# W_k's loads on another queue, W_o's low parts on another engine, projections one step earlier, the last tile in halves

## What is computed

```
x = x + o_mod(attention(k_mod(x)))     # q = k = v = x * style_k @ W_k.T * demod + b, 16 heads of 32
                                       # scores between the heads of one token, not between tokens
x = x + x @ (U V)[:-1] + (U V)[-1]     # weight of rank 30, made from cond by W_dec
x = x + clip(mod(x, W_2), -256, 256)   # a third modulated product
x = x + LN(silu(cat @ W1 + b1) @ W2 + b2) * g + be
#   cat = [h, t, m, n, r, s], each weighted: two chained LNs with gathered rows (h), two LNs with
#   gathered rows (t, s), x plus the output of a small MLP (m, n, r)
```

## Time and profile before

| what | value |
|---|---|
| three runs | 1007.46, 1013.16, 1014.13 us; median 1013.16 |
| the profiled execution | 1011.57 us, its span 1009.8 us |
| PE, DVE, ACT, POOL busy | 979.1, 662.7, 489.9, 693.9 us |
| DMA engines in 0 to 33 us | busy 0.97, 304 GB/s |
| PE busy in 61 to 70 us | 9.00 of 9 us |
| PE busy in 375 to 400 us | 24.56 of 25 us |
| POOL's om waits for DVE's om, 33 to 110 us | 13.5 us in five waits |
| first ten filler instructions of PE | 4.64 us |
| W_k's four issues on SP | 1.85 us |

### The profile page before, as it was taken

How to read it: one execution, slowest core, us unless ns; L and a number is a source line. 1 busy time by engine, 2 the same in 40 slices (tenths; PEclk the granted TensorE clock), 3 DMA queues, 4 the chain that set the end, 5 groups by cost and what they waited for, 6 DMA issues and landing times.

```text
span 1009.8 us, 18145 instructions
## 1 busy us (share of the span) xinstructions
PE 979.1 (97%) x6566; PEld 782.0 (77%) x6566; DVE 662.7 (66%) x1213; ACT 489.9 (49%) x766; POOL 693.9 (69%) x634
## 2 busy tenths in 40 slices
PE   9989999999999999899999999999999999999995
PEld 5566777777787677788888887888888888888884
DVE  6697767689868878665656557567557556664542
ACT  2798777777777545333342433233334324323231
POOL 5656676676665449777777777768768777777861
PEclk9999999999999999999999999999999999999998
DMA  9634654554422562333232332332233233223220
GB/s 280 229 121 155 226 202 148 178 208 156 143 66 64 188 221 86 107 107 120 76 107 88 109 128 86 109 115 80 81 112 111 78 96 130 66 90 107 79 76 22
DMA packets 58269, 125.10 MB, mean 124 GB/s; under 512 B 7891, under 2 KB 12117, under 8 KB 57156
## 3 DMA queue, kind: packets, MB, share of 16 engines
q1 hardware_dynamic: 46404, 81.98, 24.0%
q0 software_dynamic: 11776, 41.95, 13.4%
HBM read 105.96 MB, written 17.95 MB: 123 GB/s over the span
## 4 chain that ended last, share of the span: by engine, by line
PE 73%; POOL 9%; issue 6%; DVE 6%; DMA 3%; ACT 2%; SPq 1%; POOLq 0%; DVEq 0%; ACTq 0%
PE ps L592 36%; PE ps_y L599 7%; PE ps_k L680 7%; PE ps_o L599 5%; PE tp L604 4%; PE ps_v L633 2%; PE ps_s L665 2%; PE ps_u L700 1%; PE ps_t L713 1%; DMA x_in<-in_x_turned 1%; PE tp L913 1%; POOL h L1810 1%; PE ps_vt L660 1%; DMA xb<-in_x_wide 1%; POOL tt L1818 1%
## 5 line engine op out<-in xcount | busy, mean ns | idle before, releaser
L1796 POOL TENSOR_TENSOR rstd<-var_eps,half 128x1 f32<-128x1 f32 x95 | 53.6, 564 | 105.3 <-DVE var_eps L1561 104.6
L1193 ACT ACTIVATE g_out<-ps 128x512 f32<-128x512 f32 x32 | 19.1, 597 | 170.5 <-PE ps L998 170.5
L1015 ACT ACTIVATE at_diag<-at 32x512 f32<-32x512 f32 x128 | 80.5, 629 | 18.8 <-DVE at L1354 17.5
L1740 POOL TENSOR_TENSOR om<-om,bc 128x512 f32<-128x512 f32 x32 | 41.3, 1292 | 68.1 <-DVE om L1324 68.0
L1727 POOL TENSOR_SCALAR xb<-xb,bias_o 128x512 f32<-128x512 f32 x32 | 52.9, 1652 | 43.6 <-DMA xb<-in_x_wide 43.5
L1567 DVE TENSOR_SCALAR shift_n<-mean_var,rstd 128x1 f32<-128x1 f32 x96 | 20.5, 214 | 94.1 <-POOL rstd L1796 91.8
L1015 ACT ACTIVATE k_diag<-kt 32x512 f32<-32x512 f32 x128 | 80.1, 626 | 1.1
L1147 ACT ACTIVATE h<-h,shift_n,rstd 128x512 f32<-128x512 f32 x32 | 26.1, 817 | 84.6 <-DVE shift_n L1567 84.6
L1547 DVE TENSOR_TENSOR t_lo<-tp,t_hi 128x512 fp32r<-128x512 f32 x64 | 43.8, 685 | 30.0 <-ACT t_hi L1143 30.0
L680 PE MATMUL ps_k<-wk_hi,xh 128*128 128x512 f32 x128 | 54.1, 423 | 0.6 <-DVE xl L1368 0.6
L592 PE MATMUL ps<-wx_high,x_hi 128*128 128x512 f32 x128 | 53.2, 415 | 0.0
(11 more groups left out here) (296 smaller groups left out, 3194.5 us busy)
## 6 DMA issues: line engine op xcount, KB each, us to landing
raw<-in_dec_w SPq DMA_DIRECT2D x30, 512.0 KB, 5.1
x_in<-in_x_turned SPq DMA_DIRECT2D x32, 256.0 KB, 5.0
xb<-in_x_wide SPq DMA_DIRECT2D x32, 256.0 KB, 4.7
x_dram<-xb SPq DMA_DIRECT2D x32, 256.0 KB, 3.8
xt<-x_dram SPq DMA_DIRECT2D x8, 1024.0 KB, 7.9
out<-o SPq DMA_DIRECT2D x32, 256.0 KB, 2.0
raw<-in_int_W SPq DMA_DIRECT2D x7, 1024.0 KB, 6.1
id_rows<-in_id_rows SPq DMA_DIRECT2D x32, 64.0 KB
```

What stands on the lines that cost most here:

```text
L1015: last = nc.scalar.activation(dst[g, :, q, :], src[g, :, :], ACT.Copy)
L1740: nc.gpsimd.tensor_tensor(om[:, :], om[:, :], bc[:, STYLE_O, t // TB, :], ALU.mult).then_inc(mix_step, 1)
L1796: nc.gpsimd.tensor_tensor(rstd[:, k:k + 1], var_eps[:, k:k + 1], half[:, :], ALU.pow).then_inc(norm_step[k], 1)
```

## The change

Seven edits, all in one file:

- W_k's four loads are issued by ACT in front of its first activation, and no more by SP. The memset of the ones comes first on DVE, and PE runs six filler products before the first styles instead of five (each is two instructions).
- W_o: ACT makes the high parts in steps 1 and 2, two each, before in steps 2 to 5. The low parts, and two operations of the small MLPs' LN (by gain, plus shift), go from DVE to POOL, in `prepare(3)` to `prepare(6)`.
- O_AT = 2G - 1: each projection, its xb load, bias, end and store come one step earlier. `low_o` stands ahead of kb. Two table rows (`table_rows_t(1)`) move from `prepare(7)` into step O_AT, ahead of total.
- `order()`: chunk 0 stands before attention step T+3, chunk 1 before T+4.
- The last store of x1 at the change of stages falls into the ordinary pattern.
- The last tile: b2 comes into `ps_4` by a product with the unit matrix; g_out is turned into two banks, high and low parts are made in halves of two chunks; moments are taken from `ps_4`, ACT normalizes from it in two halves of 256 columns.
- Its gain, sum and store are in halves of 256 columns too.

```
-    O_AT = 2 * G
+    O_AT = 2 * G - 1
...
+    yield "chunk", 0
     yield "attend", T + 3
-    yield "chunk", 0
+    yield "chunk", 1
     yield "attend", T + 4
...
-    yield "chunk", 1
     yield "attend", T + 5
...
-            for c in range(C):
-                sp.dma_start(w_raw[0][:, c, :], I["w_k_t"][c * P:(c + 1) * P, :]).then_inc(wk_in[c], 16)
...
+            for c in range(C):
+                act.dma_start(w_raw[0][:, c, :], I["w_k_t"][c * P:(c + 1) * P, :]).then_inc(wk_in[c], 16)
...
-            keep_busy(ps_o, 5)
+            keep_busy(ps_o, 6)
...
+            def last_out():
+                pe.wait_ge(f2_ready, T - 1)
+                pe.wait_ge(tables_in, 16 * 3)
+                nc.tensor.matmul(ps_4[:, :], ident[:, :], b2[:, :], start=True, stop=False)
+                pe.wait_ge(g_ready, T)
+                pe.wait_ge(lo_ready["g"], T - 1)
+                pe.wait_ge(lo_ready["s"], T)
+                for bank, chunks in zip(last_g, chunk_halves):
+                    for c in range(chunks.start, chunks.stop):
+                        mm = nc.tensor.transpose(bank[:, c, :], g_out[:, c * P:(c + 1) * P], ident[:, :])
+                    mm.then_inc(turned["g"], 1)
+                for j, chunks in enumerate(chunk_halves):
+                    pe.wait_ge(lo_ready["g"], T + j)
+                    for c in range(chunks.start, chunks.stop):
+                        for x, w in ((hi["g"], Wt["out"][0]), (hi["g"], Wt["out"][1]), (lo["g"], Wt["out"][0])):
+                            mm = nc.tensor.matmul(ps_4[:, :], x[:, c, :], w[:, c, :], start=False, stop=c == C - 1 and x is lo["g"])
+                mm.then_inc(l4_done, 1)
...
-                if 2 <= s < 2 + C:
+                if s in (1, 2):
                     act.wait_ge(wo_in, 16 * 2)
-                    split_high(1, s - 2)
+                    for c in range(2 * (s - 1), 2 * (s - 1) + 2):
+                        split_high(1, c)
...
+                if s == O_AT:
+                    table_rows_t(1)
...
+                if has(4) and s not in (T + 1, T + 3):
+                    low_o(s - 4)
                 if has(0):
                     dve.wait_ge(k_done, s + 1)
...
-                if has(4) and s not in (T + 1, T + 3):
-                    low_o(s - 4)
...
-                if 3 <= s < 3 + C:
-                    split_low(1, s - 3)
...
+                if 3 <= s < 3 + C:
+                    c = s - 3
+                    pool.wait_ge(wsplit_hi[1], c + 1)
+                    nc.gpsimd.tensor_tensor(wo_lo[:, c, :], w_raw[1][:, c, :], wo_hi[:, c, :].bitcast(F32), ALU.subtract).then_inc(wsplit_lo[1], 1)
+                if s == 4:
+                    pool.wait_ge(mlp_step, 12)
+                    pool.wait_ge(vec_in, 16 * 6)
+                    nc.gpsimd.tensor_tensor(mlp_h2[0:MLP_ROWS, :], mlp_h2[0:MLP_ROWS, :], vec_g[0:MLP_ROWS, :], ALU.mult).then_inc(mlp_step, 1)
...
+                    for j, cols in enumerate(column_halves):
+                        dve.wait_ge(fn_ready, T + j)
+                        nc.vector.tensor_tensor(f2[:, cols], f2[:, cols], gain[:, cols], ALU.mult).then_inc(fg_ready, 1)
+                        dve.wait_ge(fg_ready, T + j)
+                        nc.vector.tensor_tensor(o[:, cols], f2[:, cols], x3s[f % 4][:, cols], ALU.add).then_inc(o_ready, 1)
```

More of the change, by code:

```diff
@@ L572, in refine @@
                     load(g + 1)
-                if has(2):
+                if has(2) and f < T - 1:
                     sp.wait_ge(o_ready, f + 1)
                     sp.dma_start(out_tiles[f], o[:, :]).then_inc(stored, 16)
+                if f == T - 1:
+                    for j, cols in enumerate(column_halves):
+                        sp.wait_ge(o_ready, T + j)
+                        sp.dma_start(out_tiles[f][:, cols], o[:, cols]).then_inc(stored, 16)
                 if k == 3 and g + 1 == SECOND:
@@ L953, in refine @@
                     chunk(g, k if s == 0 else k - 1)
-                if has(1) and d > 0:
+                if d == T - 1:
+                    last_out()
+                if has(1) and 0 < d < T - 1:
                     turn_g(d)
@@ L974, in refine @@
                     chunk(g, 3)
-                if has(1):
+                if has(1) and d < T - 1:
                     pe.wait_ge(lo_ready["g"], d + 1)
@@ L1220, in refine @@
                     high("t", c, tp[1], l3_done, c)
-                if has(2):
-                    normalize(LN3, f, f2[:, :], f2[:, :])
+                if d == T - 1:
+                    for j, (bank, chunks) in enumerate(zip(last_g, chunk_halves)):
+                        act.wait_ge(turned["g"], T + j)
+                        act.wait_ge(l4_done, T - 1)
+                        nc.scalar.activation(hi["g"][:, chunks, :], bank[:, chunks, :], ACT.Copy).then_inc(hi_ready["g"], 1)
+                if has(2) and f < T - 1:
+                    normalize(LN3, f, f2[:, :], f2[:, :])
+                if f == T - 1:
+                    act.wait_ge(norm_step[LN3], nth(NORM, "shift", T) + 1)
+                    act.wait_ge(o_ready, T - 1)
+                    for cols in column_halves:
+                        nc.scalar.activation(f2[:, cols], ps_4[:, cols], ACT.Identity, bias=shift_n[:, LN3:LN3 + 1],
+                                             scale=rstd[:, LN3:LN3 + 1]).then_inc(fn_ready, 1)
                 if has(-1) and b > 0:
@@ L1647, in refine @@
                 if f == T - 1:
-                    dve.wait_ge(fn_ready, T)
                     dve.wait_ge(tables_in, 16 * 3)
-                    nc.vector.tensor_tensor(f2[:, :], f2[:, :], gain[:, :], ALU.mult).then_inc(fg_ready, 1)
-                    dve.wait_ge(fg_ready, T)
                     dve.wait_ge(stored, 16 * f)
-                    nc.vector.tensor_tensor(o[:, :], f2[:, :], x3s[f % 4][:, :], ALU.add).then_inc(o_ready, 1)
+                    for j, cols in enumerate(column_halves):
+                        dve.wait_ge(fn_ready, T + j)
+                        nc.vector.tensor_tensor(f2[:, cols], f2[:, cols], gain[:, cols], ALU.mult).then_inc(fg_ready, 1)
+                        dve.wait_ge(fg_ready, T + j)
+                        nc.vector.tensor_tensor(o[:, cols], f2[:, cols], x3s[f % 4][:, cols], ALU.add).then_inc(o_ready, 1)
                 if s == 0:
@@ L1665, in refine @@
                     layer2_end(g, k - 1)
-                if has(1):
+                if has(1) and d < T - 1:
                     low("g", d, tp[2])
+                if d == T - 1:
+                    for j, (bank, chunks) in enumerate(zip(last_g, chunk_halves)):
+                        dve.wait_ge(hi_ready["g"], T + j)
+                        nc.vector.tensor_tensor(lo["g"][:, chunks, :], bank[:, chunks, :], hi["g"][:, chunks, :].bitcast(F32),
+                                                ALU.subtract).then_inc(lo_ready["g"], 1)
                 if has(0):
@@ L1691, in refine @@
                     low("h", c, tp[0])
-                if has(1):
+                if d == T - 1:
+                    dve.wait_ge(l4_done, T)
+                    moments(LN3, d, ps_4[:, :])
+                if has(1) and d < T - 1:
                     dve.wait_ge(l4_done, d + 1)
```

24 lines of the change are left out of this document (9 added, 15 removed).

## The result

The changed kernel takes 1023.38 us (median of 4 runs, 1021.38 to 1027.01) against 1011.88 of the kernel before on the same chip (4 runs): a ratio of 1.0119, 95% interval 1.0089 to 1.0148. It is slower, by 11.5 us. I had forecast 1016, so the sign was right; the size was not, and 1023.38 lies 0.4 above the upper end of the range. The profiled execution took 1021.38, its span 1019.5.

A forecast was written before the change was run, and what follows sets the result against it. TensorE, busy for 979.1 of 1009.8 us, was taken to bound the kernel. Head +0.3, steady steps +4.3, change of stages +3.4 and end -3.4 summed to +4.6 on the profiled 1011.57: 1016 us, range 1006 to 1023.

The forecast's parts named there:

- Head: Opening to mixing 9: earlier W_k loads, work moved to POOL, projection 0 in step 7; +0.3 us, bounds -1.2 to +3.6.
- Steady steps: Attention steps from 11 to 31: PE newly waits for ol of the same step; +4.3 us, bounds +1.5 to +5.5.
- +2.6: Step 23: long raw-weight sums delay ol, a 3.4 us wait of which PE already waits 0.8 today.
- Change of stages: From om's last turn to LN1: PE waits for z, LN1 begins 3.4 us later; +3.4, bounds -3.2 to +4.5.
- Rival (a): Change of stages: PE ends last, so the step gives -3.2 instead of +3.4; 1008 us in total, chance 0.22.
- The end: Last tile: bias product, halves, no f, and full clock for the twelve products; -3.4 us, -1.5 with the low clock.
- -1.9 for the clock: Last tile: with PE's gaps filled or shortened, the twelve products run at full clock instead of 0.50; -1.9 us.
- -0.5 - 0.7 - 0.3 = -1.5: Last tile without clock gain: bias product and g halves -0.5, f dropped -0.7, halves of gain, sum and store -0.3.
- Rival (b): Slower: POOL's moved operations and DVE stretch each other, up to 1 us each in steps 5 to 7; 1021, chance 0.14.
- Rival (c): Opening: earlier W_k loads bring the whole pipeline forward by their 1.9 us; 1014 us, chance 0.05.

The follow-up runs named there:

- e4: Kernel before with W_k's loads on ACT's queue, six fillers, W_o's high parts earlier, its low parts and two row operations on POOL: 1009.85 us, ratio 0.9992.
- e2: Kernel before with only the projections seven steps behind, their chunk order, low_o and table-row places and dropped store: 1025.06 us, ratio 1.0133.
- e8: Changed kernel with idle products on PE, 12 ahead of step 23's wait for ol, 10 ahead of the wait for z: 1024.7 us, ratio 1.0102.
- e11: Changed kernel with step 22's raw-weight sum in step 23, ten idle products ahead of z, tile 30 normalized first: 1018.58 us, ratio 1.0067.
- e12: Changed kernel with chunks in their old places, step 22's raw-weight sum in step 23, tile 30 normalized first: 1016.50 us, ratio 1.0049.
- e1: Changed kernel without the projections seven steps behind, its other parts kept: 1012.32 us, ratio 1.0001.

## Why the prediction was wrong

The mechanism was right where it said that seven steps behind opens a wait for ol and one for z. What failed is the price of the clock and of the end. The sum put the low clock behind those two waits at nothing, and it cost 1.55 us each. It put a clock gain of 1.9 us at the end, where nothing was to be had. And it took the stretch behind the last output as fixed, where 1.7 us were lost. The parts in turn:

**Head: about right.** +0.3 forecast, -0.4 in the trace; mixing 9 lies between 95.5 and 97.2 in the seven traces with eight steps behind, so one trace can't tell the two apart. Mixing 5 began at 59.38, forecast 59.5. Step 7 paid for its projection, mixing 8 lies 1.3 later where 1.7 was forecast, and step 8 has no wait for at_diag. But one effect I missed, and it shows only over many traces. In all seven traces with seven steps behind PE waits 1.93 to 1.95 us for at_diag ahead of step 5's mixing and 1.57 to 1.61 ahead of step 7's, in all seven with eight steps 1.13 to 1.34 and 0.69 to 0.70. Ahead of step 5's mixing that isn't because at_diag comes later: it starts 6.2 us after the mixing of step 4 in e4 and in the changed kernel. low_o now stands ahead of kb, so om's turn waits less for ol, and PE reaches the mixing sooner. Two waits of 1.25 and 1.22 us have become one of 0.55 and one of 1.93, at the same sum. e4, then the changed kernel:

```profile
55.80 0.63 PE L711 MATMUL ps_t<-ident,om 128*128 128x128 f32 x4 [1.25 <-DVE ol L1295]
56.50 2.55 ACT L1015 ACTIVATE at_diag<-at 32x512 f32<-32x512 f32 x4
59.10 1.08 PE L631 MATMUL ps_v<-at_diag,v 128*32 128x128 f32 x32 [1.22 <-ACT at_diag L1015]
```

```profile
55.37 0.63 PE L714 MATMUL ps_t<-ident,om 128*128 128x128 f32 x4 [0.55 <-DVE ol L1330]
56.78 2.54 ACT L1038 ACTIVATE at_diag<-at 32x512 f32<-32x512 f32 x4
59.38 0.86 PE L634 MATMUL ps_v<-at_diag,v 128*32 128x128 f32 x24 [1.93 <-ACT at_diag L1038]
```

And in four of the seven (e2, e8, e11, e12), in none of the others, the work behind the longer wait then runs at a low clock, and mixing 5 to mixing 9 take 38.4 to 38.7 us instead of 36.8 to 36.9 (36.42 before). The changed kernel's profiled execution is one of the three that were spared. Its stretch from mixing 5 to mixing 6, and e2's (1.6 us longer):

```profile
59.40:68.20 8.80, 8.80 (x109) 6.15 (x113) 6.18 (x10) 8.52 (x15) 8.05 (x7) 1.00 0.46 151
```

```profile
60.60:71.00 10.40, 10.39 (x112) 7.31 (x116) 8.00 (x14) 9.07 (x16) 5.79 (x6) 0.84 0.41 132
```

**Steady steps: +4.3 forecast, +6.0 measured, above the bound of +5.5.** The step of the argument was right: ol of the same step, 3.0 us of wait in step 23 where 3.4 was worked out, +0.8 in step 31 as forecast, and 0.8 for 0.9 in steps 11, 15, 19 and 27. Another 0.6 lies in step 18, which takes between 10.7 and 11.5 us over the traces of both kinds. The term that was mis-sized is step 23: "+2.6" measured 3.9. With the gap filled (e8) 2.4 of that stay; the other 1.55 are the projection at half clock. I had read in the earlier trace rows what two gaps do to the clock, and used it for the end alone, where it was a gain, and not for the gaps that my own argument opened.

**Change of stages: +3.4 forecast, +5.4 measured, above the bound of +4.5.** The same omission. The wait for z is 2.40 us as forecast, the neighbours 29 and 30 cost 0.9 where 1.0 was forecast, and PE's saved projection won nothing behind LN1's statistics, as I had argued (21.4 us from there to the first one-hot in both kernels); 1.55 us is the clock behind the wait for z, as e8 shows. Rival (a) fell here: the statistics started 5.4 us later against om's turn, not less than 2. The rest, about 0.5, stays open.

**The end: -3.4 forecast, -1.2 in the trace, and +0.4 against an end at full clock.** Two errors. First, -1.9 for the clock took one execution's low clock for the kernel's: e2 and e4 have the old end at full clock, so the halves had nothing to win there. What remains, -0.5 - 0.7 - 0.3 = -1.5, measured -1.3 on the chain. Second, I never asked what lies behind the last output, and took the 3.9 us there as fixed. The moved normalization of tile 30 put POOL's last work 1.2 us later, its DRAIN of 9.25 us became the last thing to end, and 1.7 were lost. ScalarE's normalization and POOL's wait for it in the changed kernel:

```profile
1006.25 0.81 ACT L1171 ACTIVATE f<-f,shift_n,rstd 128x512 f32<-128x512 f32 x1
1007.14 1.30 POOL L1852 TENSOR_TENSOR f<-f,gain 128x512 f32<-128x512 f32 x1 [5.77 <-ACT f L1171]
```

**Sum.** On the profiled executions the steps give +9.7 against my +4.6, and the medians +11.5. The profiled execution was the fastest of its four. Of the 1.8 us between the two sums I can name one candidate, the low clock behind mixing 5, 1.6 us in four traces of seven; the other three executions have no trace, so it isn't shown.

Rival (b), the mechanism that should have made the kernel slower, acted a little and cost nothing. In e4 the four subtractions take 1.27 to 1.29 us on POOL and the two row operations 1.7, where I had taken 1.04, and DVE's xl beside them takes 1.11 to 1.32, where it was 0.65 to 1.09 in the same steps before; yet e4 is not slower. Rival (c) did not act: mixing 9 is 0.4 us earlier in the changed kernel, 1.1 earlier in e4, and 0.2 later in e1.

## What to carry to other kernels

Whoever argues that an edit opens a gap on TensorE should price the gap and what runs behind it: here waits of 2.4 and 3.0 us cost 1.55 us each on top, and in the trace with idle products in the gaps just that was gone. Two kernels' marks share what both executions happen to have, so marks want more than one trace of each kernel. A low clock seen in one execution is not a property of the kernel until another trace shows it. And the end of a kernel is a race of all engines: before shortening the last chain, look at when the others finish, with the time that their own last instruction takes.

## What the runs showed that I had not expected

- POOL's DRAIN at the end of the block takes 9.24 to 9.26 us in every trace, wherever it starts (it includes POOL's last sum of 1.3 us); DVE's takes 0.5 to 0.7, ACT's 0.8 to 1.1, SP's 0.007. In the changed kernel it begins at 1008.5, 11.0 us before the span's end, and is the last to end; in the kernel before at 996.4, 13.4 us before the end, and isn't.
- The same wait of PE is followed by a low clock in one execution and not in another: behind the 1.94 us ahead of step 5's mixing the work up to mixing 6 took 8.8 us in three traces and 10.4 in four. A trace in which it didn't happen isn't proof that it won't.
- The clock also fell with no wait ahead of it: between mixing 28 and mixing 30, in ten of fourteen traces, while the profile had PE busy all the time. Each such fall cost 1.6 us (in e1 3.1). What sets it off isn't shown.
